# Routing stage of a two-layer network: the router as stationary operand in four column groups, ranks one product earlier, the scatter split between wide passes

## The chip, the cores and the metric

One core of one Trainium2 chip runs the whole program. The metric is the device time of one execution in microseconds (us), the median of several runs. Engines: PE is TensorE (matrix products), DVE is VectorE, ACT is ScalarE, POOL is GpSimd, SP is SyncE, which here only starts transfers.

## The reference

Two layers on x of 2 x 2048 tokens x 256 channels, each with adaptive layer norm (scale and shift from a conditioning vector). Layer 0: a gated linear recurrence, then a mixture of experts. Layer 1: windowed attention, then two local-attention and gated-MLP sublayers. The change touches the first half of the mixture of experts:

```python
scores_aE = x_aD @ router_DE                       # 4096 tokens x 8 experts, 256 channels
topv_aK, topi_aK = jax.lax.top_k(scores_aE, 2)
gates = sigmoid(scores masked to the chosen two)
routed_in_EaD = x_aD[None, :, :] * gates_Ea[:, :, None]
...
shared_aF = silu(x_aD @ w_in_shared_FD.T) * (x_aD @ w_swiglu_FD.T)
out_aD = shared_aF @ w_out_shared_DF.T + sum over the two experts of the routed MLP
```

## The kernel before, in words

The program is a row of stages. `gated_recurrence` ends near 502 us, `route_tokens` (lines 877 to 1313) runs from there to about 716, and `run_experts` follows. Each engine has its own instruction list in each stage, in written order, and the engines meet through semaphores. No scheduler moves anything.

`route_tokens` does two things at once, in NBLK = 4 blocks (`it` = 0 to 3) of 2 x 512 tokens (`b` = 0, 1; four rows of 128 tokens each, so TI = 8 token tiles a block):

- *The shared expert.* `up(it, q)`, q = 0 to 7, makes one 128-wide piece of both hidden products for 512 tokens (q // 4 is b): 8 products of 512 columns in `ps`, which has two places. ACT applies `silu`, DVE multiplies (`product(it, q)`, into `hid`). `up` of number n waits for `product` n - 2. `down(it, b)` is 16 products of 256 columns (x4 quarters of the hidden width, `f`) into `pso`; DVE scales it (`output`), POOL adds it to x (`add_output`). `down(it, 1)` is put into the next block, behind `up(it + 1, 1)`. `turn(it + 1, b, k)` transposes normalised rows of the next block, behind the ups 2 to 5, ACT writes them to `hT` with scale and shift (`affine`).
- *The routing.* `scores(it)` are the router products, 16 of them: hT (128 tokens) is stationary and the 8 router columns are the moving side. On DVE `best` finds the top values and indices, `choose` marks the chosen experts (a cast, two `pick` comparisons, `chosen`), `weigh` makes the gates, `place_rows` turns the counts from TensorE (`ranks(it)`, 16 small bf16 products over `chosen`) into row numbers, `gate_rows` multiplies the rows by their gates into `gated`. `scale_rows(it + 1, b)` normalises the next block's rows. POOL's `modulate(it)` applies scale and shift to the rows themselves, in four passes over 128 x 1024 elements (lines 964, 967), and `scatter(it)` issues 16 indirect transfers of 128 rows to the sorted table (line 976).

Written order of one block before: TensorE `up 0, up 1, ranks, down(it-1, 1), up 2, turn, up 3, turn, up 4, turn, up 5, turn, down(it, 0), scores(it+1), up 6, up 7`. DVE: `product 0, product 1, weigh, place_rows, scale_rows(it+1) twice, output(it-1, 1), gate_rows(it, 0), product 2, gate_rows(it, 1), product 3, 4, statistics, product 5, output(it, 0), best(it+1), product 6, choose(it+1), product 7`. POOL: `add_output(it-1, 1), scatter(it), modulate(it+1), add_output(it, 0)`.

The waits that hold it together:

```python
pe.wait_ge(s_hid, n - 1)            # up: product n-2 has freed its place in ps
pe.wait_ge(s_chosen, it + 1)        # ranks: choose(it) is done
pe.wait_ge(norm.s_xn, it * NB + b + 1)   # turn: scale_rows(it, b) is done
dve.wait_ge(s_h, it * NB + b + 1)   # gate_rows: POOL's modulate is done
dve.wait_ge(s_sorted, it * ROUTED * 16)  # gate_rows: the last block's scatter has landed
```

## Time and profile before

| | before |
|---|---|
| median of 3 runs | 3204.3 us (3202.83 to 3207.18) |
| the profiled execution's own time | 3175.27 us |
| its span, first to last instruction | 3173.4 us |
| mean granted TensorE clock | 0.989 |
| TensorE busy | 3053.4 us (96%) |
| DVE busy | 1954.9 us (62%) |
| ACT busy | 1721.0 us (54%) |
| POOL busy | 763.4 us (24%) |

The span is taken from one profiled execution; its own time stands beside it. A matmul row of the trace counts two records for each f32 product (so `x4` of an up row are two products), and one for a transpose; the records overlap, so the rate is read from one row's start to the next row's start. The number in brackets at the end of a timeline row is the engine's idle time before it and what ended it. The granted clock is a share of 2.4 GHz.

### The profile page before, as it was taken

What the parts mean: (1) busy time and instruction counts of PE and PEld (TensorE: products, weight loads), DVE (VectorE), ACT (ScalarE), POOL (GpSimd) and SP (SyncE); (2) the same over time, 40 slices, a digit from 0 to 9 for tenths busy, and PEclk for the clock granted to TensorE, in tenths of its full rate; (3) what the DMA queues carried; (4) which work ended last, traced back from release to release, by engine and by line L of the source; (5) the groups of instructions that cost most, each with busy time, mean ns of one, the idle gap of its engine ahead of it and who ended that gap; (6) DMA issues with size and microseconds to landing.
All of it is one profiled execution on the core that took longest, in us unless ns stands there. A gap on an engine that the chain in (4) does not pass through costs nothing. (4 is left out here: it accounts for less than half of the span.)

```text
span 3173.4 us, 49527 instructions
## 1 busy us (share of the span) xinstructions
PE 3053.4 (96%) x16616; PEld 1908.5 (60%) x16617; DVE 1954.9 (62%) x4607; ACT 1721.0 (54%) x3801; POOL 763.4 (24%) x1037
## 2 busy tenths in 40 slices
PE   8999998998999989999998999999999999998999
PEld 4455556558999963333334666665555666666555
DVE  6999995653333346666664787785333777777342
ACT  6776762213333326665665888875222777776221
POOL 1111113550000035555533222221011112112111
PEclk9999999999999999999999999999999999999999
DMA  9900004013111121111101000000001000000000
GB/s 330 318 1 1 1 1 165 29 54 103 46 48 48 45 77 29 31 29 26 29 14 42 10 11 9 10 8 32 1 0 36 9 11 10 9 9 5 14 14 27
DMA packets 114255, 134.11 MB, mean 42 GB/s; under 512 B 14478, under 2 KB 100342, under 8 KB 113786
## 3 DMA queue, kind: packets, MB, share of 16 engines
q1 hardware_dynamic: 106042, 109.54, 10.6%
q0 software_dynamic: 7872, 21.77, 2.2%
q8 instruction: 117, 1.92, 0.3%
q14 instruction: 96, 0.79, 0.1%
q10 hardware_dynamic: 128, 0.10, 0.0%
HBM read 60.30 MB, written 60.83 MB: 38 GB/s over the span
## 5 line engine op out<-in xcount | busy, mean ns | idle before, releaser
L1880 DVE CUSTOM_DVE_ANT_0 sb_win_masked<-ps_win_pss,sb_win_around 128x384 f32<-128x384 f32 (+1 forms) x512 | 256.3, 538 | 167.0 <-PE ps_win_pss L2008 166.9
L2320 ACT ACTIVATE sb_loc_pr<-ps_loc_psw,sb_loc_nb,sb_loc_sc 128x256 f32<-128x256 f32 x512 | 281.0, 569 | 135.9 <-DVE sb_loc_nb L2465 135.9
L2547 PE MATMUL ps_stk_banks<-sb_stk_w,sb_loc_hT 128*128 128x512 f32 x768 | 348.3, 603 | 2.7 <-ACT sb_loc_hT L2287 2.7
L1742 ACT ACTIVATE sb_win_pT<-ps_win_pst 128x512 f32<-128x512 f32 x368 | 199.8, 596 | 167.3 <-PE ps_win_pst L2019 167.2
L1473 PE MATMUL ps_exp_ps<-sb_exp_xT,sb_exp_here 128*128 128x128 f32 x2272 | 266.8, 276 | 0.0
L1473 PEld LDWEIGHTS ps_exp_ps<-sb_exp_xT,sb_exp_here 128*128 128x128 f32 x2272 | 261.0, 193 | 0.1
L2008 PE MATMUL ps_win_pss<-sb_win_kT,sb_win_q 32*128 32x384 f32 (+1 forms) x1024 | 230.4, 520 | 31.7 <-DVE sb_win_qtok L1880 21.3
L2547 PEld LDWEIGHTS ps_stk_banks<-sb_stk_w,sb_loc_hT 128*128 128x128 f32 x768 | 141.2, 190 | 177.9 <-issue 177.9
L752 PE MATMUL ps_rec_psp<-sb_rec_hT,sb_rec_w 128*128 128x512 f32 x512 | 230.1, 592 | 0.8 <-DVE sb_keep_modf L543 0.8
L2842 DVE SCALAR_TENSOR_TENSOR sb_mlp_hid<-ps_stk_banks,sb_stk_col,sb_mlp_gl 128x512 f32<-128x512 f32 (+1 forms) x112 | 75.1, 672 | 245.5 <-ACT sb_mlp_gl L2797 245.3
L2019 PE MATMUL ps_win_pst<-sb_win_qm,sb_win_kT 32*128 32x512 f32 x736 | 211.2, 647 | 1.5 <-ACT sb_win_pT L1742 1.5
L1665 POOL TENSOR_SCALAR_AFFINE_SELECT sb_win_pT<-sb_win_pT 128x512 f32<-128x512 f32 x240 | 146.5, 634 | 244.3 <-ACT sb_win_pT L1742 244.3
L2233 POOL TENSOR_TENSOR sb_loc_t<-sb_loc_t 128x512 f32<-128x512 f32 x64 | 81.4, 1272 | 468.1 <-DVE sb_loc_t L2411 468.0
L2008 PEld LDWEIGHTS ps_win_pss<-sb_win_kT,sb_win_q 32*128 32x128 f32 x1024 | 81.7, 183 | 161.2 <-DVE sb_win_qtok L1880 148.8
L2461 DVE TENSOR_REDUCE sb_loc_top<-ps_loc_psw 128x4 f32<-128x1024 f32 x128 | 156.1, 1219 | 24.9 <-PE ps_loc_psw L2585 22.4
L752 PEld LDWEIGHTS ps_rec_psp<-sb_rec_hT,sb_rec_w 128*128 128x128 f32 x512 | 96.3, 190 | 116.5 <-issue 116.5
L1637 POOL DMA_INDIRECT sb_win_got<-expert_results,sb_keep_row x64 | 61.9, 968 | 416.5 <-POOLq L1353 401.4
L2900 PE MATMUL ps_mlp_pso<-sb_stk_w,sb_mlp_hid 128*128 128x256 f32 (+1 forms) x768 | 160.5, 383 | 0.0
L1426 DVE TENSOR_TENSOR sb_exp_hid<-ps_exp_ps,sb_exp_act_f 128x512 f32<-128x512 f32 x71 | 49.1, 692 | 169.0 <-PE ps_exp_ps L1473 169.0
L2797 ACT ACTIVATE sb_mlp_gl<-ps_stk_banks,sb_stk_col 128x512 f32<-128x512 f32 x48 | 33.0, 687 | 217.1 <-PE ps_stk_banks L2889 217.0
L2900 PEld LDWEIGHTS ps_mlp_pso<-sb_stk_w,sb_mlp_hid 128*128 128x128 f32 (+1 forms) x768 | 133.1, 189 | 28.6 <-issue 10.5
L1393 ACT COPY sb_exp_xT<-ps_exp_psx 128x256 f32<-128x256 f32 x71 | 26.4, 372 | 223.8 <-PE ps_exp_psx L1464 223.8
(362 smaller groups left out, 6725.2 us busy)
## 6 DMA issues: line engine op xcount, KB each, us to landing
sorted_tokens<-sb_rec_blank SPq DMA_DIRECT2D x9, 4224.0 KB, 30.2
sb_exp_rows<-sorted_tokens SPq DMA_DIRECT2D x71, 128.0 KB, 2.0
expert_results<-sb_exp_res SPq DMA_DIRECT2D x71, 128.0 KB, 1.7
sb_moe_w_in<-in_L_ffn_w_in_eDF SPq DMA_DIRECT2D x8, 512.0 KB, 10.7
sb_moe_w_sw<-in_L_ffn_w_swiglu_eDF SPq DMA_DIRECT2D x8, 512.0 KB, 10.8
sb_exp_w_out<-in_L_ffn_w_out_eFD POOLq DMA_DIRECT2D x8, 512.0 KB, 8.7
sb_stk_angles<-in_angles SPq DMA_DIRECT2D x32, 128.0 KB, 3.8
sb_stk_xs_b<-sb_stk_y SPq DMA_DIRECT2D x64, 63.5 KB
```

What stands on the lines that cost most here:

```text
L752: i = nc.tensor.matmul(out, w[:, k, j * REC + g * P:j * REC + (g + 1) * P], hT[:, G % 2, k], start=(k == 0), stop=(k == KD - 1))
L1473: i = nc.tensor.matmul(ps[:, k % 2, j, f * P:(f + 1) * P], here[:, k % 2, j, c * FF + f * P:c * FF + (f + 1) * P], xT[:, k % 2, c], start= ...
L1665: nc.gpsimd.affine_select(part, part, [[0, AG], [-towards, P]], ALU.is_ge, outside, base=0, channel_multiplier=towards).then_inc(s_cut, 1)
L1742: nc.scalar.activation(pT[:, n % PARTS], pst[:, n % TURNED], ACT.Exp, scale=SC).then_inc(s_e, 1)
L1880: nc.vector.tensor_tensor_reduce(masked[:, pair % 2, j, 0:keys], pss[:, (n + j) % PLAIN, 0:keys], around[:, first:first + keys], 1.0, -3e3 ...
L2008: nc.tensor.matmul(pss[:, n % PLAIN, 0:len(keys) * P], q[rows, u % RINGS, g], kT[rows, keys[0]:keys[-1] + 1].rearrange("p a n -> p (a n)") ...
L2019: nc.tensor.matmul(pst[:, n % TURNED], kT[rows, key], qm[rows, u % 2].rearrange("p g n -> p (g n)"), start=True, stop=True, skip_group_che ...
L2233: nc.gpsimd.tensor_tensor(qq, qq, t2[:, 0:INNER], ALU.add).then_inc(s_rope, 1)
L2320: e = nc.scalar.activation(pr[:, hf, h], psw[:, hf, h // 2, h % 2 * 256:h % 2 * 256 + 256], ACT.Exp, scale=sc8[:, b, hh:hh + 1], bias=nb[: ...
L2461: nc.vector.tensor_reduce(top[:, hf], psw[:, hf].rearrange("p a (h n) -> p (a h) n", h=2), AX_X, ALU.max).then_inc(s_top, 1)
L2547: t = nc.tensor.matmul(psa[:, c], hT[:, b, k, 1 - k:P + 1 - k], w[:, k, c * 512:(c + 1) * 512], start=(k == 0), stop=(k == KD - 1))
L2900: i = nc.tensor.matmul(pso[:, t], hid[at:at + M, b, f, t * P:(t + 1) * P], w2[at:at + M, f], start=(f == 0 and t % 2 == 0), stop=(f == KH ...
```

## The change

The router matrix is padded on the host from 8 to 32 columns (LANE = 32) and becomes the stationary side. For each of the two channel halves `k`, four products put 256 tokens each through one group of 32 array columns, into partitions `lane * 32` on of `psg[:, 0:256]`. ACT copies that to `lane_scores` (`copy_lanes`), two TensorE transposes bring tokens back to the partitions (`turn_scores`, into `psg[:, 256:512]`), and `best` reads from there. `scores(it + 1)` now stands in the middle of `down(it, 0)`, `turn_scores` at its end. `down` waits for `hid` quarter by quarter. `ranks(it)` moves from behind `up(it, 1)` to behind `up(it, 0)`; in block 0 it stands behind `up(0, 2)`. DVE makes `gate_rows` before `scale_rows` of the next block, and both before `output(it-1, 1)`. POOL issues the scatter in four groups of four, with its passes in between. ACT's `gates` come behind silu 0.

```diff
-                    for b in range(NB):
-                        pe.wait_ge(norm.s_hT, norm.ready(it, b))
-                        for n in range(TB):
-                            at = (b * TB + n) * EXP
-                            for k in range(KD):
-                                i = nc.tensor.matmul(psg[:, at:at + EXP], hT[:, it % 2, b, k, n * P:(n + 1) * P],
-                                                     router[:, k], start=(k == 0), stop=(k == KD - 1))
+                    pe.wait_ge(norm.s_hT, norm.ready(it, NB - 1))
+                    for k in range(KD):
+                        for lane in range(P // LANE):
+                            b, half = lane // HALVES, lane % HALVES
+                            i = nc.tensor.matmul(psg[lane * LANE:(lane + 1) * LANE, 0:2 * P], router[:, k],
+                                                 hT[:, it % 2, b, k, half * 2 * P:(half + 1) * 2 * P], start=(k == 0),
+                                                 stop=(k == KD - 1), skip_group_check=True)
+                    i.then_inc(s_lanes, 1)
+
+                def turn_scores(it):
+                    pe.wait_ge(s_lanes_here, it + 1)
+                    for j in range(HALVES):
+                        i = nc.tensor.transpose(psg[:, (2 + j) * P:(3 + j) * P], lane_scores[:, j * P:(j + 1) * P], ident[:])
...
                 def down(it, b):
-                    pe.wait_ge(s_hid, it * UF + (b + 1) * KF)
...
                     for f in range(KF):
+                        pe.wait_ge(s_hid, it * UF + b * KF + f + 1)
...
+                        if b == 0 and it + 1 < NBLK:
+                            if f == 1:
+                                scores(it + 1)
+                            if f == KF - 1:
+                                turn_scores(it + 1)
...
+                scores(0)
+                pe.wait_ge(s_shared, 16 * 3)
+                up(0, 0)
+                turn_scores(0)
                 pe.wait_ge(s_ones, 1)
                 pe.wait_ge(s_b, 16)
-                scores(0)
-                pe.wait_ge(s_shared, 16 * 3)
...
-                        if q == 1:
+                        if q == (0 if it else 2):
                             ranks(it)
-                            if it:
-                                down(it - 1, 1)
+                        if it and q == 1:
+                            down(it - 1, 1)
```

POOL's list for blocks:

```diff
                 for it in range(NBLK):
+                    settle_rows(it)
+                    scatter(0)
                     if it:
                         add_output(it - 1, 1)
-                    scatter(it)
+                    scatter(1)
                     if it + 1 < NBLK:
-                        modulate(it + 1)
+                        scale(it + 1, 0)
+                    scatter(2)
+                    if it + 1 < NBLK:
+                        offset(it + 1, 0)
+                    scatter(3)
+                    if it + 1 < NBLK:
+                        scale(it + 1, 1)
+                        offset(it + 1, 1)
                         add_output(it, 0)
```

Instruction order of TensorE at the end of block 0, before: down(0, 0) is row 223, the scores of block 1 row 224, up(0, 6) the rows behind.

```order
222 L1239 MATMUL ps_route_pst<-sb_keep_ident,sb_route_xn 128x128 x4
223 L1285 MATMUL ps_route_pso<-sb_route_w_out,sb_route_hid 128x256 x16
224 L1250 MATMUL ps_route_psg<-sb_route_router,sb_route_hT 128x8 x16
225 L1260 MATMUL ps_route_ps<-sb_route_hT,sb_moe_w_in 128x512 x2
226 L1260 MATMUL ps_route_ps<-sb_route_hT,sb_moe_w_sw 128x512 x2
```

The same place in the change:

```order
223 L1272 MATMUL ps_route_pst<-sb_keep_ident,sb_route_xn 128x128 x4
224 L1324 MATMUL ps_route_pso<-sb_route_w_out,sb_route_hid 128x256 x8
225 L1282 MATMUL ps_route_psg<-sb_route_hT,sb_route_router 32x256 x8
226 L1324 MATMUL ps_route_pso<-sb_route_w_out,sb_route_hid 128x256 x8
227 L1290 MATMUL ps_route_psg<-sb_keep_ident,sb_route_lane_scores 128x128 x2
228 L1299 MATMUL ps_route_ps<-sb_route_hT,sb_moe_w_in 128x512 x2
```

The scores stand between the two halves of down and are half as many, on 32 columns of the array; the transposes stand ahead of up(0, 6).

POOL's round of block 0, before (the scatter of block 0, then the passes for block 1; the last row is both `add_output` calls):

```order
208 L973 TENSOR_TENSOR sb_route_settle<-sb_keep_one 128x1 [waits route_rowu,route_gated]
209 L976 DMA sorted_tokens<-sb_route_gated,sb_route_rowu 38016x256 x16
210 L964 TENSOR_TENSOR sb_route_xn<-sb_route_xn,sb_layer_moe_scale_row 128x1024 [waits layer0_tr,route_settle]
211 L967 TENSOR_TENSOR sb_route_xn<-sb_route_xn,sb_layer_moe_shift_row 128x1024 [waits route_hmul]
212 L964 TENSOR_TENSOR sb_route_xn<-sb_route_xn,sb_layer_moe_scale_row 128x1024 [waits layer0_tr]
213 L967 TENSOR_TENSOR sb_route_xn<-sb_route_xn,sb_layer_moe_shift_row 128x1024 [waits route_hmul]
214 L983 TENSOR_TENSOR sb_keep_x<-sb_keep_x,sb_route_og 128x1024 [waits route_og] x2
```

POOL's round of block 1 in the change:

```order
218 L979 TENSOR_TENSOR sb_route_settle<-sb_keep_one 128x1 [waits route_rowu,route_gated]
219 L985 DMA sorted_tokens<-sb_route_gated,sb_route_rowu 38016x256 [waits route_settle]
220 L985 DMA sorted_tokens<-sb_route_gated,sb_route_rowu 38016x256 x3
221 L991 TENSOR_TENSOR sb_keep_x<-sb_keep_x,sb_route_og 128x1024 [waits route_og]
222 L985 DMA sorted_tokens<-sb_route_gated,sb_route_rowu 38016x256 x4
223 L967 TENSOR_TENSOR sb_route_xn<-sb_route_xn,sb_layer_moe_scale_row 128x1024 [waits layer0_tr]
224 L985 DMA sorted_tokens<-sb_route_gated,sb_route_rowu 38016x256 x4
225 L973 TENSOR_TENSOR sb_route_xn<-sb_route_xn,sb_layer_moe_shift_row 128x1024 [waits route_hmul]
226 L985 DMA sorted_tokens<-sb_route_gated,sb_route_rowu 38016x256 x4
227 L967 TENSOR_TENSOR sb_route_xn<-sb_route_xn,sb_layer_moe_scale_row 128x1024 [waits layer0_tr]
228 L973 TENSOR_TENSOR sb_route_xn<-sb_route_xn,sb_layer_moe_shift_row 128x1024 [waits route_hmul]
229 L991 TENSOR_TENSOR sb_keep_x<-sb_keep_x,sb_route_og 128x1024 [waits route_og]
```

Three of the passes stand singly between groups of four transfers, three stand together at the end.

DVE in block 1, before: `weigh` behind the products 6, 7, 0 and 1, then (rows 781 to 786) `place_rows`, then the next block's rows (787 to 790), then the output and the gated rows (792):

```order
786 L1150 COPY sb_route_rows<-sb_route_rowf 128x16
787 L1085 SCALAR_TENSOR_TENSOR sb_layer_nmr<-sb_layer_mv,sb_layer_rstd 128x4
788 L1091 TENSOR_SCALAR sb_route_xn<-sb_keep_x,sb_layer_rstd,sb_layer_nmr 128x256 x4
791 L1173 TENSOR_TENSOR sb_route_og<-ps_route_pso,sb_keep_gates 128x1024
792 L1159 TENSOR_SCALAR sb_route_gated<-sb_route_xn,sb_route_gate 128x256 x8
```

And in the change:

```order
786 L1176 COPY sb_route_rows<-sb_route_rowf 128x16
787 L1192 TENSOR_TENSOR sb_route_hid<-ps_route_ps,sb_route_act_f 128x512
788 L1185 TENSOR_SCALAR sb_route_gated<-sb_route_xn,sb_route_gate 128x256 x16
789 L1110 SCALAR_TENSOR_TENSOR sb_layer_nmr<-sb_layer_mv,sb_layer_rstd 128x4
790 L1116 TENSOR_SCALAR sb_route_xn<-sb_keep_x,sb_layer_rstd,sb_layer_nmr 128x256 x4
793 L1199 TENSOR_TENSOR sb_route_og<-ps_route_pso,sb_keep_gates 128x1024
```

The gated rows now stand ahead of the normalised rows of the next block, and product 1 (row 787) between `place_rows` and both.

## Rows read from the trace of the kernel before

**Rows 1.** The page, part 1: busy us (share of the span) and instructions.
```profile
PE 3053.4 (96%) x16616; PEld 1908.5 (60%) x16617; DVE 1954.9 (62%) x4607; ACT 1721.0 (54%) x3801; POOL 763.4 (24%) x1037
```

**Rows 2.** Shared weights: issue (start us, us), and from the DMA view us to landing.
```profile
506.48 0.47 SPq L949 DMA_DIRECT2D sb_route_w_out<-in_shared_out  x1
...
sb_route_w_out<-in_shared_out SPq DMA_DIRECT2D x1, 512.0 KB, 6.4
```

**Rows 3.** TensorE's timeline, first scores and first up: start us, us, instructions, [idle before].
```profile
510.07 5.38 PE L1250 MATMUL ps_route_psg<-sb_route_router,sb_route_hT 128*128 128x8 f32 x32 [2.40 <-issue]
515.30 3.62 PE L1260 MATMUL ps_route_ps<-sb_route_hT,sb_moe_w_in 128*128 128x512 f32 x4
```

**Rows 4.** TensorE by window: us, PE busy (records), granted clock, DMA share, GB/s.
```profile
512.00:514.00 2.00, 2.00 (x11) 0.50 1.06 408
```

**Rows 5.** TensorE's timeline, blocks 0 to 3.
```profile
540.46 7.07 PE L1285 MATMUL ps_route_pso<-sb_route_w_out,sb_route_hid 128*128 128x256 f32 x32
547.37 3.63 PE L1250 MATMUL ps_route_psg<-sb_route_router,sb_route_hT 128*128 128x8 f32 x32
550.86 1.96 PE L1260 MATMUL ps_route_ps<-sb_route_hT,sb_moe_w_in 128*128 128x512 f32 x4
...
565.33 2.73 PE L1260 MATMUL ps_route_ps<-sb_route_hT,sb_moe_w_in 128*128 128x512 f32 x4 [3.92 <-DVE sb_route_hid L1166]
567.85 2.87 PE L1260 MATMUL ps_route_ps<-sb_route_hT,sb_moe_w_sw 128*128 128x512 f32 x4
...
603.85 3.66 PE L1260 MATMUL ps_route_ps<-sb_route_hT,sb_moe_w_in 128*128 128x512 f32 x4
...
616.96 1.98 PE L1260 MATMUL ps_route_ps<-sb_route_hT,sb_moe_w_in 128*128 128x512 f32 x4 [0.87 <-DVE sb_route_hid L1166]
...
666.89 1.98 PE L1260 MATMUL ps_route_ps<-sb_route_hT,sb_moe_w_in 128*128 128x512 f32 x4 [2.56 <-DVE sb_route_hid L1166]
...
706.91 7.17 PE L1285 MATMUL ps_route_pso<-sb_route_w_out,sb_route_hid 128*128 128x256 f32 x32 [1.41 <-DVE sb_route_hid L1166]
```

**Rows 6.** DVE and POOL side by side, `choose` of block 1.
```profile
557.51 2.35 POOL L967 TENSOR_TENSOR sb_route_xn<-sb_route_xn,sb_layer_moe_shift_row 128x1024 f32<-128x1024 f32 x1
557.53 2.42 DVE L1118 TENSOR_TENSOR sb_route_pick<-sb_route_number,sb_route_topf 128x64 f32<-128x64 f32 x1
...
559.87 2.38 DVE L1118 TENSOR_TENSOR sb_route_pick<-sb_route_number,sb_route_topf 128x64 f32<-128x64 f32 x1
...
562.29 2.38 DVE L1122 TENSOR_TENSOR sb_route_chosen<-sb_route_pick 128x64 bf16<-128x64 f32 x1
```

**Rows 7.** DVE in block 0: `chosen`, first and last of `place_rows`, `scale_rows`, half of `gate_rows`.
```profile
518.27 0.23 DVE L1122 TENSOR_TENSOR sb_route_chosen<-sb_route_pick 128x64 bf16<-128x64 f32 x1
...
525.34 0.21 DVE L1135 TENSOR_TENSOR sb_route_place<-ps_route_psg,sb_route_run 128x64 f32<-128x64 f32 x1
...
526.64 0.17 DVE L1150 COPY sb_route_rows<-sb_route_rowf 128x16 f32<-128x16 f32 x1
...
526.91 1.38 DVE L1091 TENSOR_SCALAR sb_route_xn<-sb_keep_x,sb_layer_rstd,sb_layer_nmr 128x256 f32<-128x256 f32 x4
...
529.69 2.19 DVE L1159 TENSOR_SCALAR sb_route_gated<-sb_route_xn,sb_route_gate 128x256 f32<-128x256 f32 x8
```

**Rows 8.** TensorE, windowed attention: four products on four column groups, the next work.
```profile
1301.20 1.06 PE L2044 MATMUL ps_win_pso<-sb_win_pT,sb_win_v 128*32 128x512 f32 x8
1302.20 0.58 PE L2008 MATMUL ps_win_pss<-sb_win_kT,sb_win_q 32*128 32x384 f32 x1
```

**Rows 9.** TensorE, block 0: a turn, an up product (two rows), the next turn.
```profile
532.28 0.60 PE L1239 MATMUL ps_route_pst<-sb_keep_ident,sb_route_xn 128*128 128x128 f32 x4
532.71 1.88 PE L1260 MATMUL ps_route_ps<-sb_route_hT,sb_moe_w_in 128*128 128x512 f32 x4
...
536.15 0.60 PE L1239 MATMUL ps_route_pst<-sb_keep_ident,sb_route_xn 128*128 128x128 f32 x4
```

**Rows 10.** All scatter instructions: ns min/median/max; idle us ahead of them, times.
```profile
L976 POOL DMA_INDIRECT sorted_tokens<-sb_route_gated,sb_route_rowu x64: 956/960/1436, 535.0 to 706.1; - x64
...
  issue: 18.4, 61
```

More of the change, by code:

```diff
@@ L973, in scatter @@
                     nc.gpsimd.tensor_tensor(settle[:], keep["one"][:], keep["one"][:], ALU.mult).then_inc(s_settle, 1)
-                    for n in range(TI):
+                    pool.wait_ge(s_settle, it + 1)
+                def scatter(pair):
+                    for n in (2 * pair, 2 * pair + 1):
                         for c in range(2):
@@ L987, in _ @@
                 pool.wait_ge(keep["filled"], (EXP + 1) * 16)
-                modulate(0)
+                for b in range(NB):
+                    scale(0, b)
+                    offset(0, b)
                 for it in range(NBLK):
+                    settle_rows(it)
+                    scatter(0)
                     if it:
                         add_output(it - 1, 1)
-                    scatter(it)
+                    scatter(1)
                     if it + 1 < NBLK:
-                        modulate(it + 1)
+                        scale(it + 1, 0)
[6 more added lines that the diff above has]
+                        offset(it + 1, 1)
                         add_output(it, 0)
@@ L1018, in _ @@
                 norm.inverse_deviation(act, 1)
-                gates(0)
+                copy_lanes(0)
                 for it in range(NBLK):
@@ L1186, in _ @@
                 nc.vector.tensor_copy(run[:], region[:]).then_inc(s_run, 1)
+                product(0, 0)
                 best(0)
@@ L1189, in _ @@
                 weigh(0)
+                product(0, 1)
+                for b in range(NB):
+                    scale_rows(1, b)
+                product(0, 2)
+                place_rows(0)
+                for b in range(NB):
+                    gate_rows(0, b)
                 for it in range(NBLK):
                     ahead = it + 1 < NBLK
-                    product(it, 0)
-                    product(it, 1)
                     if it:
+                        product(it, 0)
                         weigh(it)
-                    place_rows(it)
-                    if ahead:
+                        place_rows(it)
+                        product(it, 1)
                         for b in range(NB):
-                            scale_rows(it + 1, b)
-                    if it:
+                            gate_rows(it, b)
+                        if ahead:
+                            for b in range(NB):
+                                scale_rows(it + 1, b)
                         output(it - 1, 1)
-                    gate_rows(it, 0)
-                    product(it, 2)
-                    gate_rows(it, 1)
+                        if not ahead:
+                            table_ends()
+                        product(it, 2)
                     product(it, 3)
-                    if not ahead:
-                        table_ends()
                     product(it, 4)
@@ L1309, in _ @@
                             down(it, 0)
-                            if it + 1 < NBLK:
-                                scores(it + 1)
                 down(NBLK - 1, 1)
```

53 lines of the change are left out of this document (31 added, 22 removed).

## The prediction

> **What bounds the kernel now.** I read the page's first part, then TensorE's timeline from 503 to 718 us, the routing stage that the change touches, then VectorE and GpSimd beside it. TensorE is busy 96% of the span [rows 1]; an edit pays only if it shortens TensorE's row of work or a wait in it. The stage runs its shared expert in four blocks (it = 0 to 3) on TensorE in written order, so each microsecond lost there moves all that follows by as much.
>
> TensorE's stage holds three kinds of loss.
> - *The scores.* 16 matmuls of 8 moving columns, each with a 128-column weight load: from 547.37 to 550.86 is 3.49 us a block [rows 5]; the first took 5.38, at a granted clock of 0.50 (1.2 of 2.4 GHz) for its larger part [rows 3, 4].
> - *Waits for `hid`*: 3.92 (block 1), 0.87 (block 2), 2.56 (block 3), 1.41 (last down product) [rows 5].
> - *Low clock.* Four records of an up product take 1.88 us warm [rows 9], and 3.62 after the first scores, 3.66 after those at 600 [rows 3, 5]. After the 3.92 wait the two fours took 2.73 and 2.87, 1.84 over warm [rows 5]. The engine had run 8-column products or stood still before each.
>
> Why `hid` is late: beside GpSimd's pass over 128x1024 elements (2.35 us) a tiny VectorE operation ends only when the pass does. `pick` took 2.42 and 2.38 and `chosen` 2.38, one per pass [rows 6], against 0.23 for `chosen` with no pass near [rows 7]. Before the change a block's five passes stand together behind 16 scatter instructions, and `choose` falls among them; the products queued behind `choose` come late, and TensorE's up(it,1) waits.
>
> **The change, part by part.** *Scores.* The router (padded to 32 columns) is now the stationary side in four column groups, the rows the moving side: 8 matmuls of 256 columns, two rounds of four groups. Nearest row: the windowed attention's 128*32 products, four column groups at once, 4 x 512 columns in 1.06 us, the next group of work starting 1.00 after its start [rows 8]. The same columns stream here, so I take 1.06; one after another they would cost 8 x 256 columns at a rate of 1.72 us per 2 x 512 (half the 3.44 of an up product [rows 9]), so 3.44. These are the bounds, 0.86 (perfect overlap, a fourth of 3.44) to 3.44. The two added transposes cost 2 of the 4 in a turn of 0.43 [rows 9]: 0.22. The ScalarE copy between them (128x256) stands beside the second half of down, 3.45 us of the 6.91 that rows 5 give, and is hidden; without that cover it costs about one 0.6 us activation. Steady saving: 3.49 - 1.06 - 0.22 = 2.21, three times: **6.6 us** (bounds -0.5 to 7.2 over the three).
> The Trainium skill (TensorEngine Tiling (Array Packing), Tiling Modes) says that changing the tiling mode drains TensorE, and gives no time; its Theoretical Speedup is up to 4x. By 4x alone the scores would be 0.86 and the sum 0.6 us better; rows 8, which hold both changes of mode, show 1.06, and the measurement is what I use.
>
> *Start.* Scores of block 0 now stand ahead of the wait for `ones` and `before`, but the first up product needs the shared weights: the last transfer is issued at 506.48 and lands 6.4 later, 512.9 [rows 2]. Up(0,0) started at 515.30 [rows 3], so it can be 2.4 earlier; the transposes behind it give 0.2 back: **2.2 us**. Its slow first half (1.7 lost) I leave as it is, since it still follows a mostly idle stretch.
>
> *Waits.* The old ones go: 3.92 + 0.87 + 2.56 + 1.41 = 8.8. The last goes because down now waits for each quarter of `hid` by itself: three quarters (5.2 us of matmuls) cover the fourth. With them go the low clock behind the 3.92 (1.84) and behind the scores at 600 (1.78), whose 8 columns become 256. Together **12.4 us**.
>
> *New waits.* These need GpSimd's round. 16 scatter instructions of 0.96 with 0.30 between [rows 10], 20.2; six passes of 2.35 [rows 6], 14.1; 0.9 for the start and the gaps: 35.2 us from the end of `gate_rows` (32.8 in block 0, one pass less). A block of TensorE is 8 x 3.44 + 1.7 (turns) + 0.4 (ranks) + 13.8 (two downs) + 1.3 (scores, transposes) = 44.7. Three passes still stand together at the round's end (scale, offset, add).
> Block 0: up(0,0) ends at 512.9 + 3.4 + 1.7 = 518.1; two more ups, silu and product give 527.4; `place_rows` 1.5 and `gate_rows` 2 x 2.2 [rows 7] end at 533.3; the last three passes run 558.8 to 566.1. Block 1 begins at 553.0, so they lie 5.8 to 13.1 into it, right on `weigh` and `place_rows`, whose two-operand steps get through one per pass: `place_rows` ends 13.8 in, product(1,1) and `gate_rows` 19.0, the first normalised rows (1.5 [rows 7]) 20.6. TensorE wants them for its turn at 17.6: wait **3.0**.
> Block 2: that lateness pushes GpSimd's last passes to 1.0 before to 6.3 after the block's start, behind `choose` (1.9 to 1.1 before): no wait. `gate_rows` then ends 13.8 in.
> Block 3: passes from 3.3 before to 4.0 after its start; `choose` starts 1.9 before, one step per pass, `chosen` at 4.1, product(2,7) at 4.8; TensorE wants ranks at 3.4 and up(3,1) at 3.8: wait **1.0**.
> Also 0.3 in block 0 (up(0,5) behind product(0,3), which now stands behind all of `gate_rows`), and half of the 1.84 of low clock for the 3.0 wait, since a wait of 2.56 cost little (1.98 against 1.88) and one of 3.92 the whole [rows 5]: 0.9. New: 3.0 + 1.0 + 0.3 + 0.9 = **5.2 us** (bounds 0.5 to 12.4, none, or as much as went).
>
> *Moved at no cost:* `ranks` before up(it,1) is covered by `choose` ending in time (where not, it is the 1.0 above); `gates` and its two table loads now lie between silu 0 and 1, and delay silu(it,1) some 0.5 us, whose product is wanted 10 us later, behind down and up(it,2). `table_ends` sits on an idle VectorE. The padded router is a few kilobytes on SP's queue, ahead of 512 KB transfers. GpSimd issues the same 64 scatter instructions, none past another engine's queue; `gate_rows` needs all of a block's scatters landed, which is 28 us into a 35 us round.
>
> *Sum:* 6.6 + 2.2 + 12.4 - 5.2 = 16.0. The profiled execution took 3175.27 for a span of 3173.4, and should become 3159.3. The median of the runs shown, 3204.3, lies 29.0 higher (0.9%); I apply the same difference to it: **3188.3 us**. All stages behind see only an earlier start.
>
> **Rivals.** A change of under 0.2% (6.4 us) can hardly be told from none.
> - *The waits only move.* For: VectorE's steps are still locked one per pass, and three passes still stand together at a phase that I know to 2 us only. Against: five stood together, and `choose` now has room up to ranks. If the new waits and clock equal the old 12.4, the gain is 8.8: 3195.5. Chance 0.17.
> - *The column groups do not overlap*, since here a second round accumulates onto the same four groups: the scores cost 3.44. Rows 8 speak against it, four groups at once into one tile. Gain 16.0 - 3 x 2.38 = 8.9: 3195.4. Chance 0.05.
> - *The phases fall well.* GpSimd's passes miss `place_rows` and `choose`, and the first up product is warm: new waits 0.5, start 1.7 better: gain 22.4: 3181.9. Chance 0.10.
> - *GpSimd becomes the bound (slower).* Its round plus what must follow it before the next, `place_rows`, product and `gate_rows` (6.6 us), is 41.8 of about 46 now. The scatter now runs beside `gate_rows`' successors, the normalising passes of VectorE. One scatter instruction took 1.436 in place of 0.960 in the trace [rows 10]. If all did, the round is 42.8 and the period 49.4: three times 3.4 lost, gain 5.8, 3198.5, no change. From a round of 39.4 it decides at all; slower by 6.4 us it is from a round of 47, 1.7 us for each instruction: at 1.8 (the round 48.6, three times 9.2 lost) 3215.9. No row is near it. Chance of no change by it 0.05, of slower 0.03.
>
> **How the numbers follow.** Forecast 0.60. The range takes in the moved waits and serial groups (3195.5) with 2 us of clock phase behind them, and 2 us below the good case (3181.9): 3180 to 3197.5. Faster by over 0.2% means under 3197.9: 0.60 + 0.17 + 0.05 + 0.10 less 0.03 for a case where both misses meet: 0.89. Same: 0.05 and this 0.03: 0.08. Slower 0.03.
>
> **What would show it.** The scores' 16 records in 1.0 to 1.2 us with a granted clock of 1.00 after them; up(0,0) starting near 512.9; a wait before a turn early in block 1 and a wait of about 1 us at ranks or up(3,1); none before the last down; the last down ending near 698 in place of 714.1; `pick` and `chosen` still at 2.4 beside a pass. It is wrong if the scores take over 2 us, if block 1 waits over 6 us, or if GpSimd's scatter instructions lengthen past 1.2 us.

## The result, and the profile after

| | before | after |
|---|---|---|
| median of four runs | 3205.2 us (3202.8 to 3207.2) | 3171.3 us (3167.7 to 3173.7) |
| profiled execution | 3175.27 | 3167.70 |
| its span | 3173.4 | 3165.9 |

The ratio is 0.989, 95% interval 0.9874 to 0.9905: 34 us faster. I had forecast 16.0 us and 3188.3; the result lies 8.7 us below my range.

The two profiled executions differ by 7.5 us only, the medians by 34. The first number to look at is therefore not in a row at all: the profiled execution of before was 28 to 32 us faster than each timed one. Part 1 of after's page, to be read against [rows 1]:

```profile
PE 3044.9 (96%) x16560; PEld 1895.4 (60%) x16561; DVE 1947.7 (62%) x4607; ACT 1725.7 (55%) x3807; POOL 766.0 (24%) x1037
```

TensorE's timeline of after (start us, us, instructions, idle before), to be read against [rows 3, 5]:

```profile
510.83 1.07 PE L1282 MATMUL ps_route_psg<-sb_route_hT,sb_route_router 128*32 128x256 f32 x16 [1.19 <-ACT sb_route_hT L1020]
515.42 3.78 PE L1299 MATMUL ps_route_ps<-sb_route_hT,sb_moe_w_in 128*128 128x512 f32 x4 [3.52 <-DMA sb_route_w_out<-in_shared_out]
...
575.99 0.66 PE L1272 MATMUL ps_route_pst<-sb_keep_ident,sb_route_xn 128*128 128x128 f32 x4 [1.50 <-DVE sb_route_xn L1116]
...
609.22 0.20 PE L1306 MATMUL ps_route_psg<-sb_route_chosen,sb_route_before 128*128 128x64 bf16 x1 [2.33 <-DVE sb_route_chosen L1148]
...
609.82 3.63 PE L1299 MATMUL ps_route_ps<-sb_route_hT,sb_moe_w_in 128*128 128x512 f32 x4
```

The scores' records end 1.07 us after their start in every block; the first up product waits for its weights; of the old waits for `hid` none is left, and two new ones stand in blocks 1 and 2. VectorE in block 2 shows why `chosen` is late: the cast takes 2.86 us and the two `pick` 4.71 us, while GpSimd runs three passes in a row from 601.73 on [rows 6].

```profile
604.20 4.71 DVE L1144 TENSOR_TENSOR sb_route_pick<-sb_route_number,sb_route_topf 128x64 f32<-128x64 f32 x2
```

From the stage's first TensorE record to that of the expert stage, before took 717.25 - 503.38 = 213.87 us, after 704.65 - 505.35 = 199.30. That is 14.6 less. The other 19 us of the result are what the experiments are about.

### The profile page after: what moved, and what is told of

The parts are those of the page before. It is cut to its first block and busy times, and to the rows that moved or that the text cites. A ratio compares the mean times of both kernels' runs of the same rounds, so it can differ in the third digit from the quotient of the medians.

```text
span 3165.9 us, 49419 instructions
## 1 busy us (share of the span) xinstructions
PE 3044.9 (96%) x16560; PEld 1895.4 (60%) x16561; DVE 1947.7 (62%) x4607; ACT 1725.7 (55%) x3807; POOL 766.0 (24%) x1037
## 5 line engine op out<-in xcount | busy, mean ns | idle before, releaser
L2945 PEld LDWEIGHTS ps_mlp_pso<-sb_stk_w,sb_mlp_hid 128*128 128x128 f32 (+1 forms) x768 | 133.1, 189 | 28.6 <-issue 10.5
## 6 DMA issues: line engine op xcount, KB each, us to landing
sorted_tokens<-sb_rec_blank SPq DMA_DIRECT2D x9, 4224.0 KB, 30.2
sb_moe_w_in<-in_L_ffn_w_in_eDF SPq DMA_DIRECT2D x8, 512.0 KB, 10.6
```

Of the source, the lines that this page charges most:

```text
L2945: i = nc.tensor.matmul(pso[:, t], hid[at:at + M, b, f, t * P:(t + 1) * P], w2[at:at + M, f], start=(f == 0 and t % 2 == 0), stop=(f == KH ...
```

## Experiments

The kernels ran in five jobs, with runs of before in each. "Routing stage" is the length just defined. One view gives a mark for what follows: the waits of VectorE, in which the output of the shared expert (`og`) waits for "remote". That is the view's word for a semaphore that was updated just before the start while no instruction or transfer known to it ended near that update; for an `og` that starts when its product is done it names TensorE instead. In the first trace of before all eight did (us in total, times, longest):

```profile
DVE sb_route_og L1173 <- PE ps_route_pso L1285: 30.3, 8, 7.3
```

How far two sets of runs of one and the same kernel differ in one job bears on every small difference below: e1 took 3212.9 us beside 3207.9 for before, and e13 3206.0 beside 3214.1 (ratio 0.9982, interval 0.9967 to 0.9998). Up to 8 us between medians is therefore no proof of a gain, whatever the interval says.

### Job 1: which part, and is the first trace typical?

**Before as it is (e1).**


> The kernel before, unchanged, to get its trace beside its ordinary time. Theory A (the profiled execution at 3175.3 was not like the timed ones near 3205, and the ordinary ones lose some 29 us somewhere): about 3205, ratio 1.000, and a trace whose span is 3190 to 3205; its stages, set beside the first trace, show where the 29 us lie. Theory B (all timed runs are alike in the trace and only the time around the span differs): a span of about 3173 and a time of 3205.


3212.9 us (before of the same job: 3207.9), routing stage 744.24 - 505.75 = 238.5 us, 24.6 more than in the first trace. The first trace was not a typical one. Of the 24.6 us TensorE stands still for 12.5 (28.1 us of idle time for 15.5); the rest is slower running, at a mean granted clock of 0.88 in the stage, for 0.97. The span is 37.5 us longer: another 10.5 lie in the windowed attention of layer 1 (602.8 for 592.4 us, clock 0.96 for 0.98). Waits of VectorE in the stage, then TensorE in the scores of block 1:

```profile
DVE sb_route_og L1173 <- remote: 52.9, 4, 15.5
```

```profile
552.65 2.41 PE L1250 MATMUL ps_route_psg<-sb_route_router,sb_route_hT 128*128 128x8 f32 x21
...
558.79 0.60 PE L1250 MATMUL ps_route_psg<-sb_route_router,sb_route_hT 128*128 128x8 f32 x3 [1.95 <-issue]
...
563.06 3.54 PE L1260 MATMUL ps_route_ps<-sb_route_hT,sb_moe_w_in 128*128 128x512 f32 x4
```

The scores need no new data and yet stand still five times in this stretch, for up to 1.95 us, and end 10.4 us after their start instead of 3.5 [rows 5]; the up product behind them runs at half clock (3.54 against 1.88). VectorE's `og`, whose products end at 552.82 by the profile, starts at 562.36, 9.5 us late. From 540.30 to 561.44 GpSimd's chain of 16 scatter instructions and its packets last; the last instruction starts at 559.39. `og` follows after 15.5 us of standing still:

```profile
562.36 1.22 DVE L1173 TENSOR_TENSOR sb_route_og<-ps_route_pso,sb_keep_gates 128x1024 f32<-128x1024 f32 x1 [15.53 <-remote]
```

The trace also holds the times of the semaphore updates, and they say what is late: TensorE's signal for this product is recorded at 562.33 only, and `og` starts 0.03 us behind it. It is the same in every wait on "remote" in the routing stages of all traces: the signal is one of TensorE's, recorded 2.2 to 10.6 us after the product's end, and the waiting engine starts within 0.1 us of it. The ends of products are modelled in the profile, so whether the product itself or only its signal is late can't be told. GpSimd's passes are not what delays it: the first of them starts at 560.37, after TensorE's pauses have begun.

In blocks 2 and 3 `og` starts 3.7 and 2.3 us after the last scatter instruction's start, after 14.89 and 13.43 us. Over the stage TensorE stands still 16.8 us in the scores (2.4 of them ahead of the first, as in [rows 3]) and 5.8 before the last down product (1.41 in [rows 5]); the first of the two, in total, times and longest:

```profile
PE ps_route_psg L1250 <- issue: 16.8, 15, 2.4
```

**Padded router input alone (e3).**
```
-router = m.sb("router", [P, KD, EXP])
+router = m.sb("router", [P, KD, LANE])      # scores still use 0:EXP
```


> Only the router's input is the padded 32-column array, in its place among the inputs; the products still use 8 columns of it and no order changes. If the gain beyond the forecast comes from where the inputs lie in memory: 3188 or less. If it comes from the routing stage's own order, or from the first trace not being typical in another way: 3205, ratio 1.000.


3213.2 us, ratio 1.0005 [0.9989, 1.0022], stage 239.6, og waits 55.8 us for "remote". Where the inputs lie in memory is not it.

**Column-group scores alone (e4)**, at the old place behind the whole down product, with ScalarE's copy and the two transposes.
```
-psg[:, at:at + EXP], hT[..., n * P:(n + 1) * P], router[:, k]
+psg[lane * LANE:(lane + 1) * LANE, 0:2 * P], router[:, k], hT[..., half * 2 * P:(half + 1) * 2 * P]
+copy_lanes(it + 1); turn_scores(it + 1)
```


> The kernel before with the scores in four column groups and the transposes, at the old place, nothing else. The forecast's terms: 3 x 2.2 less a wait for the ScalarE copy of about 0.8 each, plus the low clock behind narrow scores (1.8), plus up to 2 at the start: 6 to 9 us faster, 3196 to 3199, and the routing stage 6 to 9 us shorter in the trace. If narrow products cost more clock in ordinary executions than in the first trace: 15 to 25 us faster.


3204.3 us, ratio 0.9985 [0.9971, 0.9999]: 3.6 us below before and 8.6 below e1, the same kernel as before; the stage is 232.3 us, 6.2 shorter than in e1. So the clearest measure of these scores by themselves is the stage's, near the 6.6 that they should save. TensorE has one gap of 0.33 us left in the scores, but ScalarE's copy, whose product ended at 547.75 by the profile, starts at 557.18, behind a signal of TensorE's at 557.16, and the transposes wait 9.86 us for it. The waits of ScalarE and VectorE in the stage:

```profile
ACT sb_route_lane_scores L1020 <- remote: 46.6, 3, 16.5
DVE sb_route_og L1184 <- remote: 54.4, 4, 16.3
```

So it does not take TensorE's 8-column scores: with TensorE idle its signals are as late (9.4 us here), and VectorE and ScalarE wait for them. Nothing shows that these two engines are held themselves.

**Scatter in groups of four alone (e5)**: before with the change's GpSimd order.
```
-scatter(it)                    # 16 in a row
-modulate(it + 1)
+scatter(0); add_output(it - 1, 1); scatter(1); scale(it + 1, 0)
+scatter(2); offset(it + 1, 0); scatter(3); ...
```


> The kernel before with the scatter in four groups between the passes, nothing else. The forecast: the waits only shift, since the last three passes still stand together: 0 to 5 us faster, with waits of 1 to 4 us at up(it,1). If the five passes standing together are what costs the ordinary runs more than the first trace shows: over 10 us faster.


3189.2 us, ratio 0.9937 [0.9918, 0.9956]: the split alone gives 19 us. No wait on "remote" is left, the stage takes 219.7 us, 18.8 less than in e1; what is left are waits of 5.5 us for `hid` and a mean clock of 0.93 in the stage. I had put 0 to 5 us on the split, with waits that only shift.

### Job 2: is it the chain?

Before took 3208.8 us here.

**The changed kernel again (e2).**


> The changed kernel as it is, once more. Theory A (supply): the 13 us of the change's gain that the first trace of before does not explain lie in waits of TensorE, VectorE and ScalarE beside the scatter's chain of 16 transfers, which the changed kernel does not have in any execution: about 3171 us (3167 to 3176), ratio to before 0.989 on this chip too, and a trace in which no scores matmul shows a gap that nothing released and the routing stage takes about 196 us. Theory B (the traces differ by chance, and the extra gain lies outside the routing stage): the ratio holds, but a second trace shows the routing stage within 3 us of what the first trace of before showed, 210.7 us, and another stage shorter.


3165.7 us, ratio 0.9867 [0.9846, 0.9887], stage 198.6: theory A, 1.3 us below its range. Of waits on "remote" there are 6.0 us on ScalarE and 3.8 on VectorE, none of which reaches TensorE:

```profile
546.35 0.37 ACT L1036 COPY sb_route_lane_scores<-ps_route_psg 128x256 f32<-128x256 f32 x1 [5.97 <-remote]
```

```profile
688.59 1.23 DVE L1199 TENSOR_TENSOR sb_route_og<-ps_route_pso,sb_keep_gates 128x1024 f32<-128x1024 f32 x1 [3.78 <-remote]
```

Both stand where the change does not cut the chain into fours. In block 0 there is no `add_output` between the first two groups, so eight scatter instructions stand in a row (534.8 to 544.7), and TensorE's signal for the scores comes 2.4 us late. In block 3 there are no passes, so twelve stand in a row (671.4 to 687.0), and the signal for down comes 3.0 us late. The same pair is in after's trace and in e14; beside groups of four no trace has a wait on "remote" (one signal, of ranks in e2's block 1, comes 1.7 us late there and delays nothing).

From e1 to e2 the span falls by 47.0 us: 39.9 in the routing stage, 5.9 in the windowed attention (602.8 to 597.0), which the change does not touch.

**The change without the split (e6)**: groups of 4 and 12.
```
+scatter(1); scatter(2); scatter(3)
 scale(it + 1, 0); offset(it + 1, 0); scale(it + 1, 1); offset(it + 1, 1)
```


> The changed kernel with the scatter in a group of 4 and one of 12 (block 0: 16 in one), then the passes; all else as in the changed kernel. Theory A (a long chain of transfers starves the other engines): waits come back, 3183 to 3200 us, ratio 0.993 to 0.998 and the rows show VectorE or ScalarE idle for over 5 us until a point within 1.5 us of the last packet of the scatter. Theory C (it is the dense 8-column scores beside the chain that starve TensorE, and the change took those away): about 3171 us as the changed kernel, ratio 0.989.


3179.1 us, ratio 0.9911 [0.9890, 0.9932]: 13.4 us above e2, a little better than theory A's range. The mark is back; 30.2 us of the waits stand in block 0, where the chain is 16 long in this kernel, and 19.1 beside the chains of twelve:

```profile
ACT sb_route_lane_scores L1034 <- remote: 28.2, 3, 12.9
...
DVE sb_route_og L1197 <- remote: 21.1, 2, 17.3
```

5.0 of the 13.4 us are in the routing stage (203.6), 5.3 in the windowed attention (602.3 against 597.0), which the edit does not touch. There TensorE's idle time is 2.8 us less than in e2 and its mean clock lower (0.96 for 0.97), so this goes with the clock and not with waits; why the clock is lower, I do not explain.

**The change with 8-column scores (e7).**
```
-psg[lane * LANE:...], router[:, k], hT[..., half * 2 * P:...]      # copy and transposes gone too
+psg[:, at:at + EXP], hT[..., n * P:(n + 1) * P], router[:, k, 0:EXP]
```


> The changed kernel with the 32 matmuls of 8 columns for a block's scores in the place of the column groups, the copy and the two transposes; scatter in groups of four, ranks and VectorE's order as in the change. Theory A (the split cures the waits): each block's scores cost 3.5 us where they cost 1.07 + 0.69 us, so 4 x 1.8 = 7 us more, and the first, at half clock, 2 to 4 more: 3178 us (3175 to 3183), ratio about 0.9915. Theory C (dense scores are what starves): over 3190 us, with gaps that nothing released between the scores' matmuls.


3174.4 us, ratio 0.9889 [0.9865, 0.9913], stage 206.4: 8.6 us above e2 (12 expected), 7.9 of it in the stage, with no gap in the scores. Theory C falls, and the column groups are priced, the first block's included.

**Before with half the scatter (e8)**: only first choices.
```
-for c in range(2):
+for c in range(1):
```


> The kernel before, in which only each token's first choice is scattered (the rows of second choices are left out, so that the chain of transfers is 8 long instead of 16; the expert blocks run as often as before). Theory A: a chain of 8 lasts 10 us instead of 20 and starves little: 3180 to 3190 us, as with the split alone (3189), ratio about 0.993; GpSimd is free 10 us earlier, which shortens nothing that was on the path. Theory D (GpSimd's time or the order of its passes is the cause, and the chain's length is not): the same as before within 0.2%, 3205 us.


3181.4 us, ratio 0.9911 [0.9891, 0.9932], stage 213.6, no wait on "remote". Theory D's number (3205) is missed. The run halves the chain, the bytes and GpSimd's time at once, though, and the waits for `hid` of [rows 5] go as well, but the 1.41 before the last down; so it does not show by itself that the length is what counts. Nor do its chains of eight clear every eight: e2's block 0 has a late signal beside one.

### Job 3: other splits, on a job of another kind

Before took 3181.6 us here, 26 and 27 us less than in jobs 1 and 2, and no trace of this job has a wait on "remote".

**Finer split (e9)**: 3, 2, 2, 3, 3, 3 transfers ahead of the six passes.
```
-scatter(3); scale(it + 1, 1); offset(it + 1, 1); add_output(it, 0)
+scatter(7, 8, 9); scale(it + 1, 1); scatter(10, 11, 12); offset(it + 1, 1); scatter(13, 14, 15); add_output(it, 0)
```


> The changed kernel with the scatter cut finer: 3, 2, 2, 3, 3 and 3 transfers before GpSimd's six passes of a block, so that no two passes stand together either. Theory A: two waits are left in the changed kernel's routing (1.5 us at a turn of block 1, 2.3 us and half a clock's 3.5 us at the ranks of block 2, where choose runs beside three passes in a row); with transfers between the passes VectorE's choose meets at most one pass, the ranks wait goes, and no new one comes: 3160 to 3167 us, 1 to 6 us below the change on one chip (3165.7). Rival E: the passes of the next block end up to 3 us later and turns wait for them: 3168 to 3175.


3155.3 us (3152 to 3159), ratio 0.991 [0.9893, 0.9928], the lowest of all, stage 191.9. In block 2 `choose` finds one pass instead of three (596.43 to 598.80), the two `pick` behind it take 0.36 us instead of 4.71, and the wait at ranks is gone; the one turn waits 0.62:

```profile
598.90 0.36 DVE L1148 TENSOR_TENSOR sb_route_pick<-sb_route_number,sb_route_topf 128x64 f32<-128x64 f32 x2
```

**Two groups of eight (e10)**: before, with the first pass between.


> The kernel before with its scatter in two groups of eight, GpSimd's first pass between them. Theory A, in the form that the other engines stop only once about ten or more transfers stand in a row: near the split in fours, 3182 to 3190 us (ratio 0.992 to 0.995). In the form that the stall grows with every transfer of a chain: half of the way, 3192 to 3200 us. Theory D (only the place of the passes counts, since e5 gave the first pass earlier): as e5, 3183 to 3189.


3191.0 us, ratio 1.0027 [1.0008, 1.0046], stage 222.5. With no late signals to cure, it only moves the passes, and TensorE waits 8.0 us for `hid`. It says nothing of the length of chain that brings them.

**Pause until landed, passes behind (e11, e17).**
```
+if n % 2 and n + 1 < TI: pool.wait_ge(s_sorted, (it * TI + n + 1) * 32)
```


> The kernel before, its passes where they were (all after the scatter), but after every four transfers GpSimd waits until they have landed. This separates a pause in the chain from the passes that the split puts there. Theory A (what starves the others is transfers of GpSimd standing in a row in its queue): as the split, 3183 to 3192 us, although GpSimd's passes start some 4 us later; VectorE and ScalarE show no wait over 8 us that ends with the scatter. Theory D (the passes come too late behind the scatter, and the split cures that): 3205 to 3215 us.


3171.3 us, ratio 0.9984 [0.9958, 1.0011]. Its ten runs fall in two groups, six from 3166.6 to 3172.0 us and four from 3187.1 to 3201.8; the traced one is of the first (no wait on "remote", stage 208.7). What the slower four lost is not traced. Undecided.

**A pause in the windowed stage's ten gathers (e12).**
```
 gather(u)
+if u == 1: pool.wait_ge(s_got[u], 32)
```


> The changed kernel, and in the windowed stage, whose GpSimd begins with ten gathers in a row, a wait until they have landed after the fourth and after the sixth. The same supply trouble seems to stand there: that stage took 592.4 us in the first trace of before, 602.8 and 601.0 in two others, 596.6 and 597.0 in the changed kernel's. Theory A: 592 to 594 us for the stage, 2 to 4 us below the changed kernel, 3161 to 3164. Rival: those 4 to 10 us are the start's clock or its loads: no difference within 2 us, 3164 to 3168.


3162.1 us, ratio 0.9933 [0.9913, 0.9953]. The windowed stage took 597.3 us, as in the changed kernel without the pause (597.3 in e18): the median lies in theory A's range, but the stage that the pause should have shortened is the same, so the rival's reading holds and the pause gives nothing. The routing code is the changed kernel's, and its stage took 195.4 us.

### Job 4: all on one chip

**Before (e13), the change (e14), the split alone (e15), the finer split (e16).**


> The kernel before, third trace. So far its median was 3208 us on the chip of the first eight experiments and 3182 on that of the next four. Theory F (on some chips the scatter's chain starves TensorE, VectorE and ScalarE, on others hardly; the mark in the trace is VectorE's output waiting for something remote, 53 us in four waits where the median was 3208, and none in the traces of the other): if this job's median of before is over 3200, the trace shows these waits and a routing stage of 230 us or more; if it is under 3190, none of them and 213 to 222 us. Rival G (each execution draws it anew): the marks and the median do not go together.

> The changed kernel, third trace, on one chip with the others of this call. Theory F: 3162 to 3172 us on either kind of chip, since only 9 us of its waits are of that kind, and these beside other work: ratio to before 0.987 to 0.990 where before is over 3200, 0.993 to 0.996 where it is under 3190, which is where my forecast of 16 us would have been right. Rival G: a ratio of 0.989 on any chip.

> The scatter split alone once more (ratio 0.9937 where before took 3208). Theory F: on a starving chip 3183 to 3191 again; on the other kind no gain, since its routing stage took 219.7 us where the first trace of before has 213.9: 3180 to 3190 us, ratio 0.999 to 1.003. Rival: the split gains 15 us or more everywhere.

> The changed kernel with the finer split, now beside the changed kernel on one chip. Routing stage 192 us where the changed kernel has 195.4 to 199.3: 4 to 8 us below it, 3152 to 3165 us, on either kind of chip. Rival (the 3155 us were only that chip): within 2 us of the changed kernel.


Before took 3214.1 us in this job (ten runs) and 3206.0 in e13's own seven, and the waits are there (`og` waits 48.6 us for "remote", in four waits; routing stage 235.0 us), as theory F wants.

The change: 3166.9 us, ratio 0.9855 [0.9839, 0.9872], stage 198.6. The split alone: 3190.3 us, 0.9936 [0.9915, 0.9956], again without a wait on "remote", but its stage takes 226.6 us, only 8.4 less than e13's, with 8.7 us of waits for `hid`; another 11.6 us are in the windowed attention (594.1 for 605.7). The finer split: 3162.3 us, 0.9842 [0.9826, 0.9859], stage 193.7: 4.5 us below the change by the medians and 4.9 by the stage, though the intervals overlap and same kernels differ by more in this job. Its traced execution took 3170.1 us, 1.6 more than e14's (3168.4): its windowed attention took 605.2 us at a mean clock of 0.95, for 599.4 at 0.97.

### Job 5: the change in a job without these waits

**Pause again (e17), the change again (e18).**


> The kernel before, its passes all behind the scatter, GpSimd waiting after every four transfers until they have landed; last time on a chip where before took 3182 us. On a chip where before takes over 3200: theory A (transfers in a row starve the others; a pause cures that, and passes in the pause are not needed) expects 3166 to 3192 us and no wait of VectorE's output on anything remote over 8 us; theory D (only passes in between cure it) expects 3195 us or more with four waits of 12 us or more on something remote. On a chip where before takes under 3190: 3165 to 3190 again, and nothing is decided.

> The changed kernel, fourth trace. Theory F: on a chip where before takes over 3200, 3163 to 3172 us and a ratio of 0.986 to 0.990; on one where before takes under 3190, 3157 to 3168 us and a ratio of 0.992 to 0.996. Rival G (the gain is the same on each chip): 0.986 to 0.990 in either case.


Before took 3178.2 us. The change took 3163.2, ratio 0.9951 [0.9934, 0.9968]: **15.1 us**, and no wait on "remote"; VectorE's output now waits for TensorE and nothing else:

```profile
DVE sb_route_og L1199 <- PE ps_route_pso L1324: 29.4, 6, 7.2
```

The pause took 3173.8 us, 0.9995 [0.9969, 1.0020], with runs in two groups again (seven from 3165.4 to 3177.4, three from 3190.2 to 3195.0), and stays undecided. Theory F was right that the gain has two sizes (e14's ratio lies a little below its 0.987 to 0.990) and wrong on the chip: jobs 1, 2 and 5 ran on a chip of the same number, with before at 3207.9, 3208.8 and 3178.2. By the medians of before it goes by the job. But the first profiled execution of before (3175.27) does not fit the timed ones of its kernel (3202.8 to 3207.2), and the pause's runs differ by some 20 us within a job, so that single executions can differ too is not excluded. What sets it I don't know.

## Why the prediction was right in its parts and wrong in its number

The step that failed is the last of the sum: "The median of the runs shown, 3204.3, lies 29.0 higher (0.9%); I apply the same difference to it." I took 29 us for something outside the stage, which the change would leave. e1, e3 and e13 show 21 to 26 us more in the routing stage than the trace I worked from (235.0 to 239.6 us for 213.9), as waits and low clock beside the scatter's chain, and the change removes all but 3 to 4 of them (198.6 in e2 and e14, 195.2 in e18). The sentence "All stages behind see only an earlier start" failed with it, by less: the windowed attention took 601.0 to 605.7 us in these traces of before, 592.4 in the first, and 596.6 to 599.4 in the change's, at lower clocks where it was longer. A profiled execution 0.9% below the timed ones should have been a rival of its own: "the timed runs hold waits that this trace lacks, and they are in the part that the change rewrites". The diff held a hint: it breaks a chain of 16.

Against an execution of the same kind, the first trace of before and e18, the sum stands: the stage went from 213.87 to 699.38 - 504.20 = 195.18, by 18.7 us where I had 16.0. That the medians of job 5 differ by 15.1, so near to 16.0, is in part luck: between these two traces the windowed attention is 4.9 us longer (597.3 for 592.4), and the whole spans differ by 12.4.

- *Scores, 6.6:* 6.2 to 6.8. A block's scores take 1.00 and the transposes 0.22 from start to start, three times 2.27 saved. From down's start to the next up's start it is 8.33 us where rows 5 have 10.40, three times 2.07: the two halves of down take 3.55 and 3.56 us, 0.1 each over half of the 6.91 in rows 5. Whether that is the change of tiling mode (rows 8 held only the one behind their group, not both) or down's wait for each quarter is not separated. (An `up` is four products of 512 columns, not the eight told ahead of the prediction: its two rows have eight records. The sum took its rate from the rows, so nothing hangs on it.) e18:

```profile
538.00 3.62 PE L1324 MATMUL ps_route_pso<-sb_route_w_out,sb_route_hid 128*128 128x256 f32 x16
541.55 1.07 PE L1282 MATMUL ps_route_psg<-sb_route_hT,sb_route_router 128*32 128x256 f32 x16
542.55 3.72 PE L1324 MATMUL ps_route_pso<-sb_route_w_out,sb_route_hid 128*128 128x256 f32 x16
546.11 0.38 PE L1290 MATMUL ps_route_psg<-sb_keep_ident,sb_route_lane_scores 128*128 128x128 f32 x2
546.33 1.88 PE L1299 MATMUL ps_route_ps<-sb_route_hT,sb_moe_w_in 128*128 128x512 f32 x4
```

  "The column groups do not overlap" is dead in all blocks: two rounds of four cost what rows 8 show for one of 512 columns.
- *Start, 2.2:* 2.7, from the stage's first record to up(0,0) (9.23 against 11.92 us); it waits for the weights, as said. In absolute time up(0,0) did not start "near 512.9" but at 515.42 in the first trace of after, since that stage began 2.0 us later and the weights came with it, and its slow part was longer there (3.78 and 3.02 us, for 3.62 and 1.88).
- *Old waits and clock gone, 12.4:* gone in all traces of the change. The half clock behind a wait can return: 609.82 above took 3.63, in e18 the same product 1.98.
- *New waits, 5.2:* about 3.8 in e18 (1.41, 2.28 and 0.10 of clock), 5.6 in after's trace (1.50, 2.33 and 1.75). The turn in block 1 waits 1.4 to 1.5, not 3.0. With it half as late, GpSimd's three passes stay later against block 2, and `choose` of block 2 falls on them: 2.3 us at ranks there, where I had none, and none in block 3, where I had 1.0. "Three passes still stand together at a phase that I know to 2 us only" was fair, and that the sum of the new waits came near is in part luck, since they fell on other places; the finer split removes what they cost.
- *GpSimd as the bound:* never near. The median of its scatter instructions stayed at 0.96 us; the longest of 64 took 1.50 in e18, as one had taken 1.44 in [rows 10].

Rival G, one gain for every job, falls by e14 beside e18 (0.9855 and 0.9951, intervals apart).

How much of the gain is whose, where the signals are late: the split alone gives 18.7 us in job 1 and 23.7 in job 4, column-group scores alone 3.6 by the medians (6.2 by the stage), all together 34 to 47. The parts do not add up. Short scores beside an unbroken chain only move the wait to their copy (e4), and the split without the change's other moves keeps 5.5 to 8.7 us of waits for `hid` and a clock of 0.92 to 0.93 in the stage, for 0.97 in e2; which of the other moves gives that back was not run. Where the signals are not late the split was not run alone; the stages of e5 and e15 (219.7 and 226.6) against the first trace's 213.9 let one expect no gain from it there.

## What to carry to other kernels

Compare the profiled execution's time with the timed ones before summing durations; if they differ by more than the edit is worth, the trace lacks part of what is to be forecast, so leave room for it on the side on which the edit could remove it. Do not let GpSimd issue more than a few indirect transfers in a row beside dense work of TensorE: breaking up chains of 16 gave 19 and 24 us in the two jobs with late signals where it was run alone, though whether the gap or the pass in it does it was not separated. Put its wide passes between them, one at a time, which also keeps VectorE's two-operand steps from meeting several passes (the finer split: 3155.3 us with before at 3181.6, 3162.3 with 3214.1). A score with 8 moving columns is better turned round, with the padded router as the stationary side (here 1.22 us a block for 3.49, with 0.2 more around it), if other work covers the copy. And read a stage that an edit does not touch beside the one that it does: here it moved by up to 13 us with the granted clock.

## What was not expected of the hardware

- Beside 16 indirect transfers in a row TensorE's signals to VectorE and ScalarE came up to 10.6 us after the ends of their products (9.5 for `og` in e1, 9.4 for the copy in e4), TensorE paused between matmuls of one group for up to 1.95 us, and all went on about when the last packets had left. For shorter chains the runs give no clean rule. Beside groups of two to five there was no wait on "remote"; beside eights none in e8, e5 and e15, but a signal 2.4 us late in the change's block 0 (e2); beside twelves signals 2.3 to 4.2 us late in e6, e2, e14 and after's trace, and no wait on "remote" in e5's and e15's block 3. The core's DMA engines were not full then: from 553.0 to 562.5 in e1 the window view gives them a share of 0.27, with a granted clock of 0.66 for TensorE:

```profile
553.00:562.50 9.50, 4.38 (x29) 0.66 0.27 97
```

- Whether this happens goes mostly by the job, for one and the same kernel: before at 3208, 3209 and 3214 us where traces show it, at 3182 and 3178 in jobs whose traces show none. What makes the signals late is open. The Trainium skill (SBUF — State Buffer, Who interferes with whom) says that a DMA never contends with a compute engine; by that the data path is no candidate; the runs can't show that, only that the waits come and go with the chain. Its page Runtime: NRT & Kernel Launch, Instruction fetch mechanics, has each sequencer load its next instructions by DMA, mostly hidden; an instruction load queued behind the scatter's packets would fit the picture, but the DMA view of e1 shows only two instruction queues and no load of theirs between 538 and 574 us, which speaks against it, as far as the view is complete. Nor was it tried whether a pause alone, without a pass in it, cures the waits: both runs of that edit fell on jobs whose traces show none.
